# Cross attention on one core: the last head group by key tiles over four PSUM banks, its output products in banks of their own

## The reference

```python
text, ip_h = encoder_hidden_states[:, :end_pos], encoder_hidden_states[:, end_pos:]
q = _split_heads(hidden_states @ w_q, HEADS)
k = _split_heads(text @ w_k, HEADS)
v = _split_heads(text @ w_v, HEADS)
out_text = _merge_heads(_sdpa(q, k, v))                  # softmax over 1593 keys
k_ip = _split_heads(ip_h @ w_k_ip, HEADS)
v_ip = _split_heads(ip_h @ w_v_ip, HEADS)
out_ip = _merge_heads(_sdpa(q, k_ip, v_ip, mask=mask_ip))  # softmax over 8 keys
out = (out_text + out_ip) @ w_out + b_out + hidden_states
```

## Time and profile before

| | us |
|---|---|
| three runs, median (lowest, highest) | 1868.95 (1867.57, 1875.44) |
| the profiled execution | 1865.82 |
| its span | 1864.0 |
| PE busy | 1826.1 (98%) |
| DVE busy | 1336.9 (72%) |
| ACT busy | 1193.0 (64%) |
| POOL busy | 380.4 (20%) |

### The profile page before, as it was taken

The page is one execution under the profiler, slowest core; times in us unless marked ns, Lnnn a source line. Parts: engine busy times, 40 slices in busy tenths (PEclk is TensorE's granted clock), DMA queues, the critical chain, the costliest instruction groups (busy, mean ns, idle before and its releaser), DMA issues.

```text
span 1864.0 us, 42319 instructions
## 1 busy us (share of the span) xinstructions
PE 1826.1 (98%) x17536; PEld 729.7 (39%) x17536; DVE 1336.9 (72%) x1705; ACT 1193.0 (64%) x2352; POOL 380.4 (20%) x475
## 2 busy tenths in 40 slices
PE   8999999999999999999999999999999999999997
PEld 4333343433344443343434433334333443344332
DVE  5778777687777867677776777767777677776861
ACT  1267666666666766666666666666666666666774
POOL 5112212212112211122211211112121112121000
PEclk9999999999999999999999999999999999999998
DMA  8545344353445444364443644436344363443300
GB/s 233 87 87 160 72 77 98 68 155 74 80 94 136 85 95 84 73 157 86 85 93 71 155 85 81 93 70 167 71 82 85 70 168 73 77 101 67 83 18 24
DMA packets 99761, 178.00 MB, mean 95 GB/s; under 512 B 42853, under 2 KB 71062, under 8 KB 95826
## 3 DMA queue, kind: packets, MB, share of 16 engines
q1 hardware_dynamic: 78578, 133.89, 37.2%
q0 software_dynamic: 18976, 40.10, 6.7%
q10 hardware_dynamic: 2016, 1.31, 0.2%
HBM read 117.57 MB, written 48.82 MB: 89 GB/s over the span
## 4 chain that ended last, share of the span: by engine, by line
PE 94%; DVE 4%; DMA 1%; issue 1%; ACT 0%; SPq 0%; POOLq 0%; POOL 0%; ACTq 0%; DVEq 0%
PE pv_bank L775 25%; PE max_bank L711 22%; PE work_bank L553 12%; PE work_bank L586 11%; PE exp_bank L759 10%; PE work_bank L607 3%; PE work_bank L564 3%; PE max_bank L722 2%; DVE tile_max L1046 2%; DVE tile_max L1039 1%; PE exp_bank L763 1%; PE work_bank L592 1%; PE work_bank L618 1%; PE work_bank L576 0%; DMA ctxt<-in_ctx_t 0%
## 5 line engine op out<-in xcount | busy, mean ns | idle before, releaser
L947 ACT ACTIVATE probs<-exp_bank 128x512 f32<-128x512 f32 x1896 | 995.4, 598 | 448.0 <-PE exp_bank L759 438.7
L1046 DVE TENSOR_REDUCE tile_max<-max_bank 128x2 f32<-128x1024 f32 x632 | 774.3, 1225 | 393.0 <-PE max_bank L711 388.1
L711 PE MATMUL max_bank<-k_stack,q_stack 48*128 48x512 f32 x1896 | 561.6, 465 | 14.3 <-DVE tile_max L1046 11.4
L775 PE MATMUL pv_bank<-probs,v_ones 128*17 128x512 f32 x3840 | 513.6, 599 | 0.1
L1048 DVE TENSOR_REDUCE tile_max<-max_bank 128x1 f32<-128x512 f32 x632 | 430.3, 681 | 0.8 <-PE max_bank L711 0.8
L759 PE MATMUL exp_bank<-q_stack,k_stack 50*128 50x512 f32 x1896 | 410.3, 401 | 2.5 <-DMA q_stack<-neg_rows 1.3
L711 PEld LDWEIGHTS max_bank<-k_stack,q_stack 48*128 48x128 f32 x1896 | 234.3, 184 | 408.7 <-issue 250.4
L553 PE MATMUL work_bank<-ctxt,wk 128*32 128x400 f32 x2528 | 253.5, 506 | 7.2 <-DMA wk<-in_w_k 5.1
L759 PEld LDWEIGHTS exp_bank<-q_stack,k_stack 50*128 50x128 f32 x1896 | 236.7, 187 | 43.6 <-ACT probs L947 29.9
L586 PE MATMUL work_bank<-wv,ctxt 128*32 128x320 f32 x3040 | 246.9, 434 | 0.0
L1247 POOL DMA_DIRECT2D sums<-o_sum x39 | 27.5, 705 | 668.1 <-ACT o_sum L887 668.1
(11 more groups left out here) (121 smaller groups left out, 875.7 us busy)
## 6 DMA issues: line engine op xcount, KB each, us to landing
k_stack<-scratch_k SPq DMA_DIRECT2D x234, 200.0 KB, 6.7
scratch_k<-k_parts SPq DMA_DIRECT2D x80, 400.0 KB, 4.7
ctxt<-in_ctx_t POOLq DMA_DIRECT2D x28, 800.0 KB, 11.1
q_stack<-scratch_q SPq DMA_DIRECT2D x240, 64.0 KB, 2.3
scratch_q<-q_parts SPq DMA_DIRECT2D x80, 128.0 KB, 5.6
r_wide<-scratch_r POOLq DMA_DIRECT2D x39, 256.0 KB, 5.3
xres<-in_x SPq DMA_DIRECT2D x8, 640.0 KB, 6.7
out<-xres SPq DMA_DIRECT2D x32, 160.0 KB, 2.0
```

The costliest lines, as they stand in the source:

```text
L711: nc.tensor.matmul(round_place(n, r)[:, k, :], exact(q_stack[stack, slot, c, t * 128:(t + 1) * 128]), exact(k_stack[stack, slot, c, chunk ...
L775: last = nc.tensor.matmul(pv_bank[h * 32:h * 32 + VW, :], v_ones[:, v_slot(b, kt), head * VW:(head + 1) * VW], p, start=(kt == 0), stop=(k ...
L947: nc.scalar.activation(dst, exp_place(group_no, at), ACT.Exp, scale=SCALE).then_inc(probs_ready, 1)
L1046: nc.vector.reduce_max(flat[:, at:at + 2], place[:, 0:2, :], AX.X).then_inc(max_taken, 1)
```

## The change

Only group 39 and what follows it are changed.

The exp tiles of group 39 go by key tiles: visits 0 to 11 have four tiles each, visit 12 has the two of the rest. They rotate over four banks, the three of `exp_bank` and `max_bank` 0 (`LAST_RING`). The PV of key tile v - 1 is in visit v; visit 0 has, as before, the last PV of group 38. The two banks `max_bank` 1 and 2 and later `work_bank` are free for sums of output products: query tiles 1, 2 and 3 add up there, and nothing of them is read until the end, when `out_end` adds group 39's product onto them (`start=False`) and DVE adds each once. `LAST_OUT` says in which visit which chunk of which tile is done: chunks 3, 2 and 0 of tile 1 in visits 3 and 4, of tile 2 in 5 and 6, of tile 3 in 7 and 8, and chunk 1, which waits for the pack of group 38, in visits 9, 10 and 11. Query tile 0 does chunks 3, 2 and 0 in visits 1 and 2 in `work_bank`, and DVE adds them to `xres` at once; its chunk 1 comes after `spread_sums` in a bank of its own. `spread_sums` writes `exp_bank` 0 instead of `work_bank`.

```diff
     if last:
-        for t in range(QT):
-            put(4, ("OUT_EARLY", t), 4, (8 + 2 * t, 2), (9 + 2 * t, 2))
+        put(4, ("OUT_EARLY",), 3, (1, 1), (2, 2))
...
+LAST_RING = 4
+LAST_OUT = {3: ((1, 3),), 4: ((1, 2), (1, 0)), 5: ((2, 3),), 6: ((2, 2), (2, 0)), 7: ((3, 3),), 8: ((3, 2), (3, 0)),
+            9: ((1, 1),), 10: ((2, 1),), 11: ((3, 1),)}
+EARLY_CHUNKS, LATE_CHUNK = (3, 2, 0), 1
...
-            return (max_bank if at // BANKS % 2 else exp_bank)[:, at % BANKS, :]
+            return exp_bank[:, at % LAST_RING, :] if at % LAST_RING < BANKS else max_bank[:, 0, :]
...
-            return [] if v % 2 else [at for u in (v, v + 1) if u < VISITS for at in tiles_at(u)]
+            return list(range(v * GH, min(EXPS, (v + 1) * GH)))
...
-            return max_bank[:, t, 0:D] if t < BANKS else exp_bank[:, 0, 0:D]
+            return (exp_bank[:, 1, 0:D], max_bank[:, 1, 0:D], max_bank[:, 2, 0:D], work_bank[:, 0:D])[t]
...
+            def out_early(t, k, place, start, stop):
+
+                deep = slice(64, 97) if k == 2 else slice(0, 128)
+                for at, rows in strips(128):
+                    last = nc.tensor.matmul(place[at:at + rows, :], o_t[deep, k, ip_or_heads(k, t, at, rows)], wout[deep, k, :],
+                                            start=start, stop=stop)
+                if stop:
                     last.then_inc(work_full, 1)
...
                 for at, rows in strips(128):
-                    last = nc.tensor.matmul(bank[at:at + rows, :], o_sum[:, t * 128 + at:t * 128 + at + rows], wout_end[:, :],
-                                            start=True, stop=True)
+                    last = nc.tensor.matmul(place[at:at + rows, :], o_sum[:, t * 128 + at:t * 128 + at + rows], wout_end[:, :],
+                                            start=False, stop=True)
...
-                    last = nc.tensor.matmul(work_bank[h * 32:(h + 1) * 32, :], ident_f[:, row:row + 1].to_broadcast([128, 32]),
+                    last = nc.tensor.matmul(exp_bank[h * 32:(h + 1) * 32, 0, :], ident_f[:, row:row + 1].to_broadcast([128, 32]),
...
-                    if piece[1] == 0 and begins(turn):
+                    if begins(turn):
                         pe.wait_ge(ip_packed, B * IP_LOADS * 16)
-                    if piece[1] == 0 and turn[1] > 2:
-                        pe.wait_ge(o_packed, (B * NG - 1) * 64)
-                    out_early(piece[1], turn)
+                        pe.wait_ge(o_packed, (B * NG - 2) * 64)
+                    for n in range(turn[0], turn[1]):
+                        out_early(0, EARLY_CHUNKS[n], work_bank[:, 0:D], n == 0, n == len(EARLY_CHUNKS) - 1)
...
-                    before = n * EXPS + at - 2 * BANKS
+                    before = n * EXPS + at - LAST_RING if at >= LAST_RING else -1
...
-                        kt = PV_AT.get(v)
+                        if group_no < B * NG - 1:
+                            kt = PV_AT.get(v)
+                        else:
+                            kt = FULL if v == 0 else v - 1 if v <= FULL else None
...
+                        if group_no == B * NG - 1:
+                            for t, k in LAST_OUT.get(v, ()):
+                                if t == QT - 1 and k == EARLY_CHUNKS[0]:
+                                    pe.wait_ge(work_empty, len(PRO) + FIRST_WORK + (B - 2) * LOOP_WORK + len(work_order(False, True)))
+                                if t == 1 and k == LATE_CHUNK:
+                                    pe.wait_ge(o_packed, (B * NG - 1) * 64)
+                                out_early(t, k, out_place(t), k == EARLY_CHUNKS[0], False)
...
-            pe.wait_ge(work_empty, len(PRO) + FIRST_WORK + (B - 2) * LOOP_WORK + len(work_order(False, True)))
+            pe.wait_ge(probs_ready, B * NG * EXPS)
             spread_sums()
+            out_early(0, LATE_CHUNK, out_place(0), True, False)
...
-                            out_add(B, piece[1], number, work_bank[:, 0:D])
+                            out_add(B, 0, number, work_bank[:, 0:D])
...
-                nc.vector.reciprocal(r_wide[:, cols], work_bank[:, cols]).then_inc(spread_inverted, 1)
+                nc.vector.reciprocal(r_wide[:, cols], exp_bank[:, 0, cols]).then_inc(spread_inverted, 1)
```

More of the change, by code:

```diff
@@ L610, in out_piece, with out_end @@
                     last.then_inc(work_full, 1)
-            def out_early(t, turn):
-                for n in range(turn[0], turn[1]):
-                    k = (3, 2, 0, 1)[n]
-                    deep = slice(64, 97) if k == 2 else slice(0, 128)
-                    for at, rows in strips(128):
-                        last = nc.tensor.matmul(work_bank[at:at + rows, 0:D], o_t[deep, k, ip_or_heads(k, t, at, rows)],
-                                                wout[deep, k, :], start=(n == 0), stop=(n == 3))
-                if turn[1] == 4:
+            def out_early(t, k, place, start, stop):
[4 more added lines that the diff above has]
+                if stop:
                     last.then_inc(work_full, 1)
-            def out_end(t, bank):
+            def out_end(t, place):
                 for at, rows in strips(128):
-                    last = nc.tensor.matmul(bank[at:at + rows, :], o_sum[:, t * 128 + at:t * 128 + at + rows], wout_end[:, :],
-                                            start=True, stop=True)
+                    last = nc.tensor.matmul(place[at:at + rows, :], o_sum[:, t * 128 + at:t * 128 + at + rows], wout_end[:, :],
+                                            start=False, stop=True)
                 last.then_inc(work_full, 1)
@@ L748, in exp_tile @@
                 else:
-                    before = n * EXPS + at - 2 * BANKS
+                    before = n * EXPS + at - LAST_RING if at >= LAST_RING else -1
                 if before >= 0:
                     pe.wait_ge(probs_ready, before + 1)
-                if n == B * NG - 1 and at == BANKS:
+                if n == B * NG - 1 and at == LAST_RING - 1:
                     pe.wait_ge(max_taken, B * NG * ROUNDS)
@@ L874, in _ @@
             pe.wait_ge(o_read, B * NG)
-            pe.wait_ge(work_empty, len(PRO) + FIRST_WORK + (B - 2) * LOOP_WORK + len(work_order(False, True)))
+            pe.wait_ge(probs_ready, B * NG * EXPS)
             spread_sums()
+            out_early(0, LATE_CHUNK, out_place(0), True, False)
             pe.wait_ge(wout_end_loaded, GH * 16)
-            pe.wait_ge(probs_ready, B * NG * EXPS)
             for t in range(QT):
```

## The result

| | before | after |
|---|---|---|
| median of 14 runs each, us | 1868.91 | 1860.41 |
| lowest, highest | 1863.87, 1879.2 | 1856.55, 1872.37 |
| the profiled execution | 1865.82 | 1860.14 |
| its span | 1864.0 | 1858.3 |

The changed kernel is 8.5 us faster by the medians; the ratio is 0.9958 (95% interval 0.9941 to 0.9974). The forecast was 1858.9 and 10.1 us off, so it is right in direction and lies within the interval (0.9974 to 0.9941 is 4.9 to 11.0 us), and the measured gain falls just inside the 0.5% that I had taken as the line. The same kernel run again in a later session gave 1861.46 against 1869.82, ratio 0.9959 (0.9941 to 0.9976).

What follows compares the result with a forecast made beforehand. PE, busy for 98% of the span, was taken as the bound. 9.26 us in the last group and 0.84 in the end make 10.1 off 1868.95, so 1858.9 us; range 1855.5 to 1866.

Steps and rivals of the forecast that it cites:

- The stall and its low clock: Last group: PE's 5.17 us wait for `o_t` and 1.77 us lost at low clock behind it go, 6.94 together.
- The group: Group 39 from 1812.14 us: its visits sum to a last PV ending at 1843.99 against 1853.25, 9.26 us less.
- the ring: Group 39's four exp banks: the fourth tile waits up to 0.28 us; 0.15 taken for each of six visits, 0.90.
- The check: Group 39's 9.26 us split again: 6.94, 0.60 for the chunk that leaves, 1.7 of waits where ACT led.
- The pack: Group 38's pack lands at about 1833.6 us; PE asks for it in visit 9 at 1836.1, 2.5 us remain.
- The end: After the last PV: PE's idle time cut from 2.13 to 1.5 us, full clock taken, 0.84 us less.
- rival A: All as forecast, but the clock falls in the end as before: gain 9.3 us, 1859.7; chance 0.23.
- Rival B: PE loses time between its pieces in group 39, or the pack is late: gain 6.5 us, 1862.5; 0.28 with E.
- C: Slower: short waits in nearly every visit bring the clock to 0.50 in visits 3 to 12: 1882 us; chance 0.03.
- D: The waits of the last group's first part vanish as well: gain 12 us, 1857; chance 0.04.
- E: The wait for the pack is still there, in visit 9; gain still over 5 us; chance 0.28 together with Rival B.
- The line at 0.5%: Whole kernel: 9.3 us can be told from no change, line at 1859.6; chances faster 0.50, within 0.47, slower 0.03.

Runs made afterwards that it cites:

- the kernel with the last chunk ahead: Changed kernel with tile 0's last chunk ahead of the spreading of the sums instead of behind it; 1860.77 against 1867.65 us, ratio 0.9958.
- the kernel with chunk 2 moved: Changed kernel with a tile's chunks in the order 3, 0, 2 instead of 3, 2, 0; 1858.49 against 1867.65 us, ratio 0.9952.
- the change with fillers: Changed kernel plus small unread matmuls at the ends of groups 37 and 38 of the last batch; 1856.71 against 1867.65 us, ratio 0.9941.
- the kernel with later turns: Kernel before with only the output products' visits later, two visits on, tile 3 all in visit 16; 1863.36 against 1869.22 us, ratio 0.9977.

## Why the prediction held, and where it was off

**The stall and its low clock, 6.94 us: right.** No wait for `o_t` is left, and moving one chunk ahead of the pack brings back 6.73 us of wait and all of the loss. The size holds for the profile that it was read from; with a stall of 4.34 us the same kernel's group was 1.1 shorter.

**The group, 31.85 us forecast, 33.60 measured at full clock: the term that was mis-sized.** The step is the sum over the visits. Visit by visit, from starts in the profile of the kernel with the last chunk ahead, whose group 39 is that of the change at full clock:

| | forecast, without the ring | measured |
|---|---|---|
| visits 0, 1, 2 | 1.61, 3.06, 2.77 | 1.65, 3.11, 3.10 |
| visits 3, 5, 7 | 2.13 each | 2.18 to 2.19 |
| visits 4, 6, 8 | 2.73 each | 3.22 to 3.23 |
| visits 9, 10, 11 | 2.07 each | 2.18, 2.42, 2.18 |
| visit 12 and the last PV | 2.72 | 2.73 |
| the ring | 0.90 | in the visits above |
| all | 31.85 | 33.60 |

The ring's total came out, though not its parts. In visits 4, 6, 8 and 10, each behind a visit of 2.2 us, the exp tiles hold up the PV for 0.89 us instead of 0.66 as in the others, 0.23 each, 0.92 in all. I had charged 0.15 six times, once for visit 12, which has no fourth tile. The 1.75 us are in the pieces as I priced them. Four exp tiles take 0.66, not 0.60, where nothing waits. The PV is followed by chunk 2 after 0.98 instead of 0.87, and chunks 2 and 0 take 1.35 instead of 1.26: 0.20 in each of four visits. A chunk 1 by itself takes 0.65 instead of 0.60. Visit 2 adds 0.13 in its exp tiles. My prices came from batches of six exp tiles, from a PV in front of a deep chunk and from chunks in pairs. The new order has 13 batches of exp tiles for nine and most chunks alone or beside other neighbours. That part of each price is the passage from one kind to the next fits these rows, and the kernel with chunk 2 moved shows it for one passage (0.98 became 0.87); for the others it is not tested apart.

Two numbers beside the sum need an answer. The check gave 1.7 us to waits that go from the first stretch; its own figures, 3.1 less 1.0 and 0.90, give 1.2, and the remaining 0.5 comes from pricing 11 of the 14 PVs at 0.87. And PE's busy time, 15.56 of the first stretch's 15.64 us, leaves only the stall with its low clock and the chunk that moves out of the group to be won: 6.94 + 0.60 = 7.5, the very number by which the group got shorter. That is a coincidence of this sum and no proof that the stretch held no waits: the dearer passages took back what the waits gave.

**The pack: right, with more room.** It lands about 22.4 us after the group's first exp tile and is asked for after 28.3, 6 us of room where I had 2.5, because PE is slower than forecast. DVE's reciprocal does stand behind the addition, by nothing but 0.41 us from start to start, and it costs nothing.

**The end, 0.84 forecast, 0.68 in the profile of the change: right there, and partly by luck.** The reason given holds, as the table of the ends shows: the clock stayed up in six of the eight profiles with the shorter idle time, and in none of the four with 2.13 us. In the other two the clock fell and the end was 0.2 us longer than before, which is rival A and slightly worse. Over the eight the end gains some 0.4 us on average, about half of what I took.

**The sum.** 41.11 - 33.60 = 7.5 and 0.7 make 8.2 against 10.1, or 7.1 with the shorter stall; the medians gave 8.5 and 8.4. The forecast is within what the runs allow, but by the stages its 10.1 us were too much by 2 to 3. Rival B, at 6.5, had the right cause (switches between kinds, beside the ring's fourth tile) and more than its size. A happened in two of eight ends. C did not happen: in all three profiles that entered the group at full clock with the change's order in it, the group took 33.60 us at 1.00. D and E did not happen.

**The line at 0.5%.** It was well placed for the gain that I forecast and left the question at even odds. I had no term for the 2.18 us by which this profiled execution was later at the start of the group. It is no cost of the change: it comes and goes.

## What to carry to other kernels

In a tail where one transfer is late, order the work by when its operands land, and give each sum that must stay open a bank of its own; with 20 exp tiles queued behind one early matmul, the wait of one was the wait of all. Price a new order by its passages between kinds of work as well as by its pieces, from rows that have the same neighbours. Before measuring changes of 0.5%, see whether the spread of the runs goes with their mean clock: under 3 us of unread matmuls, most of it beside waits, brought the range of the kernel before from 13 us to 2 and its median down by 5.7. And look at a second profile of the same kernel before a difference of under 1 us in one stretch is put down to an edit; here the second profile of the change had another end.

## What the runs showed of the hardware

The granted clock fell to 0.50 in stretches in which PE was never idle: 6.07 us of 6.07 busy at 1808.25 in the changed kernel, behind two short waits of 0.45 us for ACT and 0.38 for DVE. In the twelve profiles the stretches at low clock lie at or near the ends of just those groups where only exp tiles and the 48-deep maxima stand between PVs, apart from those behind the wait for the pack, those at the program's end and one in a prologue. They come in some executions and not in others of the same kernel (at 156 to 160 us in the first profile of the changed kernel, not in its second), and they were in none of the 11 cases where 128-deep matmuls had been put there. The fillers also took the place of short waits: ahead of the last group the profile of the change with fillers has neither the 0.45 nor the 0.38. The first stretch of the earlier trace rows, with 3.1 us of waits in 15.64 by my sum, an estimate, kept 1.00. Whether the waits or the shallow matmuls bring it down was not tried apart.

An idle time of 2.13 us near the end was followed by the low clock in four profiles of four, one of 1.59 in two of eight, and the stall of 1.62 in the kernel with later turns was too (0.90 behind it).

A PV was followed after 0.87 us by a chunk 128 rows deep (1848.47 to 1849.34), after 0.98 by chunk 2, 33 rows deep (1825.55 to 1826.53 in the changed kernel), and after 0.98 by an exp tile, 50 rows deep (1822.01 to 1822.99 in the kernel with chunk 2 moved). Depth is not all of it, since a PV was followed by another PV, as deep as itself, after 1.01 (1851.19 to 1852.20).
